# Loading a 0/1 adjacency matrix in 512 x 1024 pieces instead of 128 x 4096 tiles, in a graph attention kernel

## What is computed

```python
s_i = x @ attn[:128]; s_j = x @ attn[128:]
e = leaky_relu(s_i + s_j.T, negative_slope=0.2)
e = e + where(adj > 0, 0.0, -1e9)
y = x + softmax(e, axis=1) @ x
out = (y - mean(y)) / sqrt(var(y) + 1e-5)
```

## Time and profile before

| what | us |
|---|---|
| median of 3 runs | 293.76 (292.42 to 295.58) |
| the profiled execution, device time | 294.91 |
| its span, from the first to the last instruction | 293.0 |
| TensorE matmul busy in the span | 249.6 (85%) |
| VectorE busy | 238.3 (81%) |
| ScalarE busy | 175.6 (60%) |
| memory read / written | 69.27 MB / 2.10 MB |

### The profile page before, as it was taken

How to read it: one execution, slowest core, us unless ns; L and a number is a source line. 1 busy time by engine, 2 the same in 40 slices (tenths; PEclk the granted TensorE clock), 3 DMA queues, 4 the chain that set the end, 5 groups by cost and what they waited for, 6 DMA issues and landing times.

```text
span 293.0 us, 5284 instructions
## 1 busy us (share of the span) xinstructions
PE 249.6 (85%) x2113; PEld 243.1 (83%) x2113; DVE 238.3 (81%) x391; ACT 175.6 (60%) x243; POOL 45.9 (16%) x74
## 2 busy tenths in 40 slices
PE   5970004999799999999999999999999999999960
PEld 5620004999699999999999999999999999999960
DVE  0781117946999998999899999989998999899741
ACT  1679955399556775777577656765576468230410
POOL 3000000000000220032002200320022002269210
PEclk9995555899999999999999999999999999999995
DMA  6999999999999999999999999999999991100101
GB/s 203 316 320 322 230 288 285 308 256 256 283 306 304 289 289 334 298 300 297 332 295 290 291 336 293 281 289 329 287 273 275 318 265 34 39 0 3 36 0 41
DMA packets 21275, 71.75 MB, mean 245 GB/s; under 512 B 2992, under 2 KB 3376, under 8 KB 21248
## 3 DMA queue, kind: packets, MB, share of 16 engines
q1 hardware_dynamic: 10240, 34.80, 41.3%
q10 hardware_dynamic: 10048, 34.67, 41.2%
q0 software_dynamic: 960, 1.90, 2.4%
HBM read 69.27 MB, written 2.10 MB: 244 GB/s over the span
## 4 chain that ended last, share of the span: by engine, by line
PE 69%; DVE 3%; issue 0%
PE psum L741 69%; DVE weights L624 1%; DVE x_raw L567 0%; DVE mask_t L519 0%; DVE half_moments L588 0%; DVE moments L591 0%; DVE rden L560 0%; DVE x_raw L599 0%; DVE worst L654 0%; DVE rden L554 0%; DVE worst L573 0%; DVE worst L614 0%; DVE again L656 0%; DVE rstd L596 0%
## 5 line engine op out<-in xcount | busy, mean ns | idle before, releaser
L741 PEld LDWEIGHTS psum<-xj,weights 128*128 128x128 f32 x2048 | 231.7, 194 | 31.6 <-issue 30.3
L741 PE MATMUL psum<-xj,weights 128*128 128x129 f32 x2048 | 232.4, 277 | 29.8 <-DVE weights L624 29.8
L624 DVE SCALAR_TENSOR_TENSOR weights<-q_row,r_j,mask_t 128x512 f32<-128x512 f32 x256 | 172.4, 740 | 1.2
L361 ACT ACTIVATE mask_bytes<-adj_in,sig_bias 128x4096 uint8<-128x4096 int32 x31 | 114.8, 3708 | 66.4 <-DMA adj_in<-in_adj_dram 66.3
L519 DVE STREAM_TRANSPOSE mask_t<-mask_bytes 128x1024 uint32<-128x1024 uint32 x32 | 39.6, 1238 | 27.3 <-ACT mask_bytes L361 27.3
L292 POOL TENSOR_SCALAR neg_mean<-total 128x4 f32<-128x4 f32 x7 | 4.0, 569 | 151.6 <-ACT x_raw L369 151.6
L301 POOL DMA_DIRECT2D out_dram<-x_raw x28 | 14.5, 521 | 32.1 <-ACT x_raw L383 31.9
L294 POOL TENSOR_SCALAR variance<-square_sum 128x4 f32<-128x4 f32 x7 | 12.3, 1750 | 44.4 <-ACT unused L376 44.4
L383 ACT ACTIVATE x_raw<-x_raw,offset,rstd 128x128 f32<-128x128 f32 x28 | 11.5, 480 | 11.5 <-POOL offset L298 11.5
L369 ACT ACTIVATE x_raw<-x_raw 128x128 f32<-128x128 f32 x28 | 8.2, 294 | 5.7 <-DVE x_raw L567 5.7
L376 ACT ACTIVATE unused<-x_raw,neg_mean 128x128 f32<-128x128 f32 x28 | 10.8, 388 | 0.8 <-POOL neg_mean L292 0.8
(11 more groups left out here) (56 smaller groups left out, 59.7 us busy)
## 6 DMA issues: line engine op xcount, KB each, us to landing
adj_in<-in_adj_dram SPq DMA_DIRECT2D x64, 512.0 KB, 11.7
adj_in<-in_adj_dram ACTq DMA_DIRECT2D x64, 512.0 KB, 12.9
out_dram<-x_raw POOLq DMA_DIRECT2D x28, 64.0 KB, 6.8
x_raw<-in_x_dram SPq DMA_DIRECT2D x8, 128.0 KB, 4.9
x_raw<-in_x_dram ACTq DMA_DIRECT2D x8, 128.0 KB, 5.7
out_dram<-x_raw SPq DMA_DIRECT2D x4, 32.0 KB, 1.6
attn_j<-in_L_gnn_attn_dram POOLq DMA_DIRECT2D x1, 64.0 KB, 5.5
out_dram<-x_raw ACTq DMA_DIRECT2D x4, 16.0 KB, 1.6
```

Of the source, the lines that this page charges most:

```text
L361: nc.scalar.activation(mask_bytes[:, t % BYTE_SLOTS, :, :], adj_in[:, t % ADJ_SLOTS, :, :], ACT.Sigmoid, bias=sig_bias[:], scale=200.0).th ...
L624: nc.vector.scalar_tensor_tensor(weights[:, slot_of(n, c), 0:(stop - first) * P].rearrange("p (s i) -> p s i", i=P), q_row[:, first * P:st ...
L741: return nc.tensor.matmul(banks[t % 8][:, 0:D1], weights[:, slot_of(n, c), (t - first) * P:(t - first + 1) * P], xj[:, c, 0:D1], start=(c ...
```

## The change

The adjacency is loaded in *pieces* g = (n, u): the 512 rows of block n times a quarter u of the chunks (eight chunks, 1024 columns, 256 of each quadrant's). A piece has as many bytes as a tile had, 2 MiB, and 32 pieces are loaded. In a partition stand 4 x 4 rows of 256 columns, so each run in memory is 1 KiB. Pieces come in the order in which the products need them, and a chunk of block n needs only the piece that holds its columns.

With that go these edits. `adj_in` has five slots, of which the products and x transposed hold the fourth and fifth at first (`PROD_SLOT`, `XT_SLOT`): piece 3 is loaded after the row maximum, piece 4 after the last s_i piece. `mask_bytes` has three slots, `mask_t` six of a piece each, `weights` twelve. VectorE converts pieces 0 and 1 itself, and transposes piece g+1 behind the sixth chunk of piece g (`TURN_AT` = 5). The residual of a block stands behind chunk 13 of the next, as one group of four tiles. ScalarE does all s_i pieces and the factors of q before its first conversion. The last eight chunks are taken tile by tile, in the last block alone. GpSimd issues the load of the first half of `attn` before its constants.

The diff, cut to its core:

```diff
-    ADJ_SLOTS = 3
-    BYTE_SLOTS = 2
-    MASK_SLOTS = 16
-    W_SLOTS = 8
-    BLOCKS = [(t, t + 4) for t in range(0, 32, 4)]
-    LAST = 4
-    RESIDUAL_AT = 2
-    TURN_AT = {n: [7, 15, 23, 29] for n in range(7)}
-    S_I_AT = {(0, 8): 7}
...
+    BLOCKS = TILES // K
+    PIECES = 4
...
+    ADJ_SLOTS = 5
+    PROD_SLOT = 3
+    XT_SLOT = 4
+    BYTE_SLOTS = 3
+    MASK_SLOTS = 6
+    W_SLOTS = 12
+    BY_DVE = 2
+    TURN_AT = 5
+    RESIDUAL_AT = 13
+    LAST = 8
...
-    S_I_BANK = [1, 2, 3, 4, 5, 6, 7, 7]
+    S_I_BANK = [3, 2, 1, 4, 5, 6, 7, 4]
+    S_I_LATE_AT = 5
...
-    adj_v = adj.rearrange("(r f b k) (q c) -> f k q b r c", r=Q, f=F, b=B, k=K, q=Q)
+    adj_v = adj.rearrange("(r f b k) (q u c) -> f u q b k r c", r=Q, f=F, b=B, k=K, q=Q, u=PIECES)
...
-        adj_in = sb("adj_in", [P, ADJ_SLOTS, Q, QC], i32)
-        mask_bytes = sb("mask_bytes", [P, BYTE_SLOTS, Q, QC], u8)
-        mask_t = sb("mask_t", [P, MASK_SLOTS, F, P, K], u8)
-        weights = sb("weights", [P, W_SLOTS, T * P], fp32)
+        adj_in = sb("adj_in", [P, ADJ_SLOTS, K, Q, RUN], i32)
+        mask_bytes = sb("mask_bytes", [P, BYTE_SLOTS, K, Q, RUN], u8)
+        mask_t = sb("mask_t", [P, MASK_SLOTS, PF, K * P, K], u8)
+        weights = sb("weights", [P, W_SLOTS, K * P], fp32)
...
+        spare = rows[:, 4, :].bitcast(fp32)
+        prod = rows[:, PROD_SLOT, :].bitcast(fp32).rearrange("p (c d) -> p c d", d=D)
+        xT = rows[:, XT_SLOT, :].bitcast(fp32)
...
-        def load_tile(queue, quadrants, t):
-
-            if t == ADJ_SLOTS:
-                queue.wait_ge(first_bytes_ready, 2)
-            elif t > ADJ_SLOTS:
-                queue.wait_ge(bytes_ready, t - ADJ_SLOTS)
+        def load_piece(queue, quadrants, g):
+
+            if g == PROD_SLOT:
+                queue.wait_ge(row_max_ready, 1)
+            elif g == XT_SLOT:
+                queue.wait_ge(s_i_in_psum, RB)
+            elif ADJ_SLOTS <= g < ADJ_SLOTS + BY_DVE:
+                queue.wait_ge(first_bytes_ready, g - ADJ_SLOTS + 1)
+            elif g >= ADJ_SLOTS + BY_DVE:
+                queue.wait_ge(bytes_ready, g - ADJ_SLOTS - BY_DVE + 1)
             for q in quadrants:
-                queue.dma_start(adj_in[B * q:B * (q + 1), t % ADJ_SLOTS, :, :],
-                                adj_v[t // K, t % K, q, :, :, :]).then_inc(adj_loaded[t % ADJ_SLOTS], 16)
+                queue.dma_start(adj_in[B * q:B * (q + 1), g % ADJ_SLOTS, :, :, :],
+                                adj_v[g // PIECES, g % PIECES, q, :, :, :, :]).then_inc(adj_loaded[g % ADJ_SLOTS], 16)
...
+            pool.dma_start(attn_i[:], attn[0:D, :]).then_inc(attn_loaded, 16)
...
+            def to_bytes(g):
+
+                act.wait_ge(adj_loaded[g % ADJ_SLOTS], 16 * Q * (g // ADJ_SLOTS + 1))
...
-                if t - 1 + ADJ_SLOTS < TILES:
-                    load_tile(act, HIGH_HALF, t - 1 + ADJ_SLOTS)
+                if g - 1 + ADJ_SLOTS < ALL_PIECES:
+                    load_piece(act, HIGH_HALF, g - 1 + ADJ_SLOTS)
...
             act.wait_ge(worst_ready, 1)
             s_i_piece(0)
             q_factors(0, 1)
+            s_i_piece(1)
+            s_i_piece(2)
             scale_xj(1)
-            scale_xj(2)
...
-            q_factors(1, 2)
-            to_bytes(1)
-            to_bytes(2)
...
-            to_bytes(5)
-            q_factors(2, RB)
-
-            for t in (6, 7):
-                to_bytes(t)
-            for g in range(NORM_GROUPS):
...
-                sum_rows(g)
-                for t in range(first + 2, min(first + 3, stop)):
-                    to_bytes(t)
...
-                for t in range(first + 4, stop):
-                    to_bytes(t)
+            load_piece(act, HIGH_HALF, PROD_SLOT)
+            for rb in range(3, RB):
+                s_i_piece(rb)
+            q_factors(1, RB)
+            load_piece(act, HIGH_HALF, XT_SLOT)
+            load_piece(act, HIGH_HALF, ADJ_SLOTS)
+            for g in range(BY_DVE, ALL_PIECES):
+                to_bytes(g)
+                if g < BY_DVE + 2:
+                    scale_xj(g)
+                if g % PIECES == PIECES - 1 and g > PIECES:
+                    sum_rows(g // PIECES - 1)
+                    sum_squares(g // PIECES - 1)
+                if g % PIECES == 0 and g > PIECES:
+                    normalise(g // PIECES - 2)
+            normalise(NORM_GROUPS - 1)
...
+            def turn(g):
+
+                if g >= MASK_SLOTS:
+                    dve.wait_ge(weights_ready, (g - MASK_SLOTS + 1) * PC)
+                if g < BY_DVE:
+                    dve.wait_ge(first_bytes_ready, g + 1)
+                else:
+                    dve.wait_ge(bytes_ready, g - BY_DVE + 1)
+                src = mask_bytes[:, g % BYTE_SLOTS, :, :, :].bitcast(u32).rearrange("p k r (f w) -> p (k r) f w", w=B)
+                dst = mask_t[:, g % MASK_SLOTS, :, :, :].rearrange("p f i k -> p f (i k)").bitcast(u32)
+                nc.vector.transpose(dst.rearrange("p f (r a) -> p r f a", a=B), src).then_inc(mask_ready, 1)
+
+            def first_to_bytes(g):
+
+                dve.wait_ge(adj_loaded[g], 16 * Q)
+                nc.vector.tensor_scalar(mask_bytes[:, g, :, :, :], adj_in[:, g, :, :, :], 0.0, None,
                                         ALU.is_gt).then_inc(first_bytes_ready, 1)
+
+            first_to_bytes(0)
...
                                     ALU.mult).then_inc(first_xj_scaled, 1)
-            dve.wait_ge(first_bytes_ready, 2)
-            turn(0, slice(0, Q)).then_inc(mask_ready, 1)
+            turn(0)
...
+                    mask_t[:, (n * PIECES + c // PC) % MASK_SLOTS, c // K % PF, :, c % K],
                     ALU.max, ALU.mult).then_inc(weights_ready, 1)
 
-            for n, (first, stop) in enumerate(BLOCKS):
-                dve.wait_ge(q_ready, min(n + 1, 2) if n < 2 else RB)
-                if n == 0:
-                    for t in range(1, stop):
-                        turn_tile(t)
-                dve.wait_ge(mask_ready, stop)
-                turned_before = stop
+            for n in range(BLOCKS):
+                dve.wait_ge(q_ready, 1 if n == 0 else RB)
                 for c in range(CHUNKS):
+                    g = n * PIECES + c // PC
+                    if c % PC == 0:
+                        dve.wait_ge(mask_ready, g + 1)
                     weigh(n, c)
                     if n > 0 and c == RESIDUAL_AT:
                         residual(n - 1)
-                    for at in TURN_AT.get(n, []):
-                        if at == c:
...
-                            turn_tile(turned_before)
-                            turned_before += 1
-            final_residual(len(BLOCKS) - 1)
+                    if c % PC == TURN_AT and g + 1 < ALL_PIECES:
+                        if g + 1 < BY_DVE:
+                            first_to_bytes(g + 1)
+                        turn(g + 1)
+            final_residual(BLOCKS - 1)
...
                 if rb == RB - 1:
-                    pe.wait_ge(s_i_ready, RB - 1)
+                    pe.wait_ge(s_i_ready, S_I_BANK.index(bank) + 1)
...
-                for c in range(CHUNKS - LAST):
-                    if (n, c) in S_I_AT:
-                        s_i_piece(S_I_AT[n, c])
-                    if n == 0 and c % SC == 0:
+            for n in range(BLOCKS):
+                last_chunks = LAST if n == BLOCKS - 1 else 0
+                for c in range(CHUNKS - last_chunks):
+                    if n == 0 and c == S_I_LATE_AT:
+                        s_i_piece(RB - 1)
...
                         else:
-                            pe.wait_ge(xj_scaled, c // SC)
+                            pe.wait_ge(xj_scaled, c // PC)
...
-                    for t in range(first, stop):
-                        if c == 0 and 0 < t < 8:
-                            pe.wait_ge(s_i_ready, min(t, RB))
-                        if c == 0 and t >= 8:
+                    if c == 0:
+                        if n == 0:
+                            pe.wait_ge(s_i_ready, 3)
+                        elif n == 1:
                             pe.wait_ge(s_i_ready, RB)
-                            pe.wait_ge(y_ready, t - 7)
+                        else:
+                            pe.wait_ge(y_ready, (n - 1) * K)
+                    for t in range(K):
                         last = product(n, c, t)
                     last.then_inc(weights_used, 1)
-                for t in range(first, stop):
-                    for c in range(CHUNKS - LAST, CHUNKS):
-                        if t == first:
-                            pe.wait_ge(weights_ready, n * CHUNKS + c + 1)
-                        last = product(n, c, t)
...
+            for t in range(K):
+                for c in range(CHUNKS - LAST, CHUNKS):
+                    if t == 0:
+                        pe.wait_ge(weights_ready, (BLOCKS - 1) * CHUNKS + c + 1)
+                    last = product(BLOCKS - 1, c, t)
+                    if t == K - 1:
```

(3 more changed lines are left out.)

104 lines of the change are left out of this document (25 added, 79 removed).

## The result

The changed kernel took 274.10 us in the median of four runs (273.31 to 275.48), the kernel before 294.36 (292.42 to 295.58, four runs): a ratio of 0.932, 95% interval 0.926 to 0.939. The forecast was 272.0. The profiled execution, the slowest of the four, took 275.48 us for a span of 273.7; the spans of all four go from 271.5 to 273.7.

A forecast was written before the change was run, and what follows sets the result against it. TensorE was taken to bound the kernel, its late start being the loss, with loads the second limit. 24.3 + (61.8 - 24.3) + 200.1 + 8.6 = 270.5 us of span, forecast as 272 us of time, range 267 to 298.

The forecast's parts named there:

- main case: Whole kernel: loads hidden and TensorE binding, 272 us, its own range 268 to 278; chance 0.55.
- First product: TensorE's start: chunk 0 needs one piece instead of four tiles, so the first product comes at 24.3 instead of 48.20 us.
- Block 0: First block: ScalarE's first conversion at 37.6 us, TensorE 3.0 us idle before chunk 14, block ends at 61.8.
- Rival 5: Block 0: piece 1 or 2 lands late or ScalarE's order costs more, block ends at 75, time 285; chance 0.06.
- The low clock: TensorE behind block 0's gap: if the clock falls, three chunks at half speed cost 2.6 us more.
- Steady part: Seven blocks after block 0: 28.59 us each by TensorE, 200.1 in all, VectorE keeping up at 28.3 a block.
- rival 4: VectorE binds: weighing takes 0.72 us a chunk instead of 0.669, a block 29.7, time 280; chance 0.06.
- The loads: Adjacency loads in 1 KiB runs: taken at 300 GB/s, bounds 239 and 321; last piece wanted at 244.7 us.
- rival 1: Loads bind mildly: 283.5 us at 280 GB/s, 293 at 270; chance 0.16 for 278 to 292.
- rival 2: Loads bind hard by the cost per run: 239 GB/s, time 326 us; chance 0.15, of which 0.12 slower.
- rival 3: Memory dislikes 1 KiB pieces at steps of 16 KiB and 16 MiB: 160 GB/s, time 468 us; chance 0.02.
- The tail: From TensorE's end to the end of the span, last eight chunks tile by tile: 8.6 us instead of 9.6.

The follow-up runs named there:

- Experiment 3: Changed kernel with block 0 waiting again for its four pieces and the last s_i piece in front of chunk 0: 291.76 us (one run).
- Experiment 5: Changed kernel with ScalarE's first conversion ahead of its loads of pieces 4 to 6: 273.95 us.
- experiment 2: Changed kernel with VectorE converting piece 2 too and ScalarE scaling xj of chunks 16 to 23 ahead of its first conversion: 275.73 us.
- experiment 6: Changed kernel with the last s_i piece in front of chunk 1 and ScalarE's first conversion ahead of its loads of pieces 4 to 6: 271.54 us.
- experiment 10: Changed kernel with the last s_i piece in front of chunk 1 and ScalarE's loads spread between its conversions and scalings: 267.06 us.
- experiment 7: Changed kernel with 34 extra idle transpositions on TensorE before chunk 14 of block 0: 274.27 us.
- experiment 11: Changed kernel with late s_i piece at chunk 1, ScalarE's loads spread, and 24 idle TensorE transpositions before the first product: 267.02 us.
- experiment 9: Changed kernel with quadrants 0 and 2 loaded by SyncE's queue, 1 and 3 by ScalarE's: 336.72 us (one run).
- experiment 8: Changed kernel with SyncE's queue issuing all loads of the adjacency and ScalarE's none: 344.89 us (one run).
- experiment 4: Kernel before with each 512 KB load cut by columns into four DMAs of 128 KB with 1 KiB runs: 292.78 us (one run).
- experiment 1: Changed kernel with its last s_i piece in front of chunk 1 of block 0 instead of chunk 5: 272.04 us.

## Why the prediction was right, and where it was off

The time came 2.1 us above the forecast of 272.0, within the range of its main case. By the profiled span it was 270.5 against 273.7, 3.2 us; that the time is nearer owes something to luck, since the profiled execution was the slowest of four. The mechanism was as forecast, and one of its terms, ScalarE's path to its first conversion, was too small by 3.7 us. Step by step:

- **First product:** forecast 24.3, measured 24.77; the conversion of piece 0 started at 19.22 instead of 18.73, as it landed. Experiment 3 shows that this step carries the gain.
- **Block 0:** eight weighings took 5.35 us as before (31.39 to 36.74). The clock fell in the gap as forecast. The conversion was forecast at 37.6 and came at 41.27, the gap at 3.0 us and was 5.84. The term that was mis-sized rests on "A DMA issue cost ACT 0.54 us for x ... and 0.40 for a tile's quadrant ..., so I do not scale it with the number of runs". I counted nothing for it in block 0, and the four issues took 6.03 us, 2.89 of them after the factors had ended at 37.08. The other 0.8 us came from the late s_i piece (ended at 33.79, forecast 33.0). Experiment 5 takes the issues from in front of the conversion and gets the forecast's gap of 3.0; experiments 2 and 6 show that the delay then falls on what comes next; experiment 10, with the late piece moved too, takes it off the path and gains 7 us of time. Rival 5 gave this a place ("ScalarE's order costs more"), with block 0 ending at 75; it ended near 65 (an estimate: 18 chunks of 0.893 and 2.0 for the clock behind 46.95).
- **The low clock:** forecast 2.6 us, and from chunk 14 to TensorE's end 261.9 - 43.2 = 218.7; measured 218.41. At 0.893 a chunk, 242 chunks are 216.1, so 2.3 us were lost, and 2.0 of them are the clock, at 0.50 until about 50.9. The table of experiment 7 bears this out: in six runs the loss follows the time at the low clock. The forecast had the reason right and the clock low for 1.2 us longer. It doesn't follow that a clock kept up would give the 2.0 back: in experiment 11, where it was kept up from the first product, most of the gain went into waits for VectorE. For the gap of the kernel after that was not tried.
- **Steady part:** 28.6 a block at the end. VectorE's denominators, one row a block:

```profile
72.22 0.16 DVE L542 TENSOR_SCALAR rden<-psum 128x4 f32<-128x4 f32 x1
99.44 0.15 DVE L542 TENSOR_SCALAR rden<-psum 128x4 f32<-128x4 f32 x1
...
210.66 0.15 DVE L542 TENSOR_SCALAR rden<-psum 128x4 f32<-128x4 f32 x1
239.25 0.15 DVE L542 TENSOR_SCALAR rden<-psum 128x4 f32<-128x4 f32 x1
```

  First 27.22 apart, VectorE at its own pace while it works up its lead (forecast 28.3), then 28.59, held by TensorE. A weighing took 0.669 us (eight in 5.35), so rival 4 falls; by its own 0.72 its block would be 29.9 and not 29.7.
- **The loads:** forecast 300 GB/s between bounds of 239 and 321; measured 348. This was outside my bounds: I took the earlier trace rows with 4 KiB runs as the best that loads can do and let only rows with more cost per run pull it down, although x, with 2 KiB runs, had moved at 338. The last conversions ended at 231.7, 34 us before TensorE. The rule of the Trainium skill that I weighed gives each packet a price beside its bytes ("Why small descriptors are slow"); from 4 to 1 KiB it would cost 7%, and the runs show 8% gained. Rivals 1 and 2 fall, and rival 3 with them, by the 348 GB/s. But I read the rule behind rival 3 too widely: the Trainium skill ("DMA: Bandwidth & Descriptors", section "Latency and other measured facts") tells of the step from one partition's row to the next one's, which is 64 KiB here; the 16 MiB lie between runs of one partition. No run here tests it. That the loads were forecast wrong did no harm to the time, since any rate that keeps them off the path gives the same.
- **The tail:** forecast 8.6, measured 8.3.

The sum: +0.5 for the start, +3.3 for the longer way to chunk 14, -0.3 behind it, -0.3 in the tail, which is 273.7.

## What to carry to other kernels

When an engine waits long at the start, look at how much data its first unit of work needs, and cut the input so that the first unit needs one piece; here that was worth all of the gain but a few us. A DMA issue on a computing engine was cheap (0.59 us) only now and then; with other loads outstanding it took what the queue takes to move one DMA. So put such issues between operations that have a lead, never in a row before the operation that others wait for. With two queues, give each one half of the partitions: that made 348 GB/s out of 238.

## What the runs showed of the hardware

- **Issues back up.** A 512 KB load of 512 runs took as little as 0.59 us to issue; with others outstanding 2.89 us in the kernel after, about 4.15 in experiment 9 and 2.43 in experiment 8. 512 KB in these times are 181, 126 and 216 GB/s; with two, two and one queue at work 363, 253 and 216, beside measured rates of 348, 238 and 226. That the issue waits for room in the queue fits this agreement, and that the same issue took from 0.59 to 4.15 us; how much room there is was not tried. The row of four at 33.91, 6.03 us, falls in the stretch in which ACT's queue moved 17 packets.
- **Shorter runs were faster:** 345 to 348 GB/s with 1 KiB in two kernels, 321 with 4 KiB, in the window of 18 to 21 us. Whether it is the size of the runs, the order of the addresses or, in experiment 4, the number of DMAs is open; runs of 512 B or 2 KiB were not tried.
- **Half of the partitions carried 213 to 238 GB/s,** 213 by one queue and 238 by two, with a DMA share of 1.09 to 1.12: a busy share near one does not mean full rate. The 213 in 36 to 39 us of the kernel after are the stretch with SP's queue, and so the lower half, nearly alone; experiments 1 and 10, which issue piece 4 before the queues run dry, keep 347 GB/s or more from 27 to 42 us. Why SP's queue got nearly everything for 3 us while ACT's loads were outstanding is open.
- **What a low clock costs depends on who waits.** Behind the gap of block 0 TensorE lost half of the time that it worked at 1.2 GHz (2.0 of 2.3 us in the kernel after, and alike in five other runs). At the start, 6 us at 1.2 GHz instead of 2.4 cost 0.5 us and not 3.0 (experiments 10 and 11), since VectorE had no lead to give.
